# A decoder layer on one core: the slot-table product one shared block sooner, the last shared block in the regular loop, five gathers set around the last two gates

## What is computed

```python
x = layernorm(x + ssm(x))          # 32 heads of a gated state-space mixer
x = layernorm(x + by_id(x, ids))   # one of 4 small experts, chosen by token id
# third part, flat = x as 1024 x 256:
logits = flat @ gate_w.T
_, top_idx = top_k(logits + expert_bias, 2)
top_w = softmax(logits)[top_idx]; top_w /= top_w.sum()
for e in range(16):
    out += combine[:, e:e+1] * (silu(flat @ wg[e].T) * (flat @ wu[e].T)) @ wd[e].T
out += (silu(flat @ sw_gate.T) * (flat @ sw_up.T)) @ sw_down.T     # shared expert
x = layernorm(x + out)
```

## Time and profile before

| | us |
|---|---|
| median of 3 runs | 654.33 |
| lowest, highest | 653.83, 656.0 |
| the profiled execution | 655.03 |
| its span, first to last instruction | 653.3 |
| TensorE matmuls busy | 625.1 (96%) |
| DVE, ACT, POOL busy | 536.3, 453.1, 460.5 |

### The profile page before, as it was taken

How to read it: one execution, slowest core, us unless ns; L and a number is a source line. 1 busy time by engine, 2 the same in 40 slices (tenths; PEclk the granted TensorE clock), 3 DMA queues, 4 the chain that set the end, 5 groups by cost and what they waited for, 6 DMA issues and landing times.

```text
span 653.3 us, 12045 instructions
## 1 busy us (share of the span) xinstructions
PE 625.1 (96%) x3545; PEld 492.3 (75%) x3545; DVE 536.3 (82%) x874; ACT 453.1 (69%) x742; POOL 460.5 (70%) x439
## 2 busy tenths in 40 slices
PE   7989999999999999999999999999999999899990
PEld 6677888878888788887888878878889787655550
DVE  6999999999999999999999999985975477742245
ACT  3768797887888978879788797897522346533365
POOL 4395889879898798987989879858670551545554
PEclk9989999999999999999999999999999999999996
DMA  4261112121131211311113111122116279268745
GB/s 164 74 260 63 66 49 94 42 91 64 49 108 45 73 64 49 113 61 52 64 49 113 64 49 64 48 99 79 72 43 160 73 173 352 75 187 258 192 129 155
DMA packets 25993, 66.66 MB, mean 102 GB/s; under 512 B 4099, under 2 KB 16899, under 8 KB 23179
## 3 DMA queue, kind: packets, MB, share of 16 engines
q1 hardware_dynamic: 23131, 58.54, 26.7%
q0 software_dynamic: 2832, 7.75, 4.6%
HBM read 58.00 MB, written 9.85 MB: 104 GB/s over the span
## 4 chain that ended last, share of the span: by engine, by line
PE 89%; DVE 5%; ACT 2%; issue 2%; POOL 1%; DMA 1%; ACTq 0%; DVEq 0%
PE ps L871 38%; PE ps L885 9%; PE ps L901 7%; PE ps L1165 5%; PE ps L886 4%; PE ps L803 3%; PE ps L821 3%; DVE conv L1730 3%; PE ps L1214 3%; PE ps L845 2%; PE ps L1155 2%; PE ps L1071 2%; PE ps L1049 1%; PE ps L910 1%; PE ps L1189 1%
## 5 line engine op out<-in xcount | busy, mean ns | idle before, releaser
L1730 DVE SCALAR_TENSOR_TENSOR conv<-ps,w_raw,conv 128x506 f32<-128x506 f32 (+3 forms) x352 | 320.7, 934 | 15.7 <-ACT conv L1373 9.4
L871 PE MATMUL ps<-x_hi,w_hi 128*128 128x512 f32 x384 | 158.9, 414 | 2.7 <-DVE x_lo L1651 1.6
L1373 ACT ACTIVATE conv<-ps,w_raw 128x512 f32<-128x512 f32 x160 | 108.4, 688 | 65.1 <-PE ps L871 64.7
L871 PE MATMUL ps<-x_hi,w_lo 128*128 128x512 f32 x384 | 151.8, 395 | 0.0
L871 PE MATMUL ps<-x_lo,w_hi 128*128 128x512 f32 x384 | 150.7, 392 | 0.0
L532 POOL TENSOR_TENSOR decay<-cum_b,cum_tok 128x512 f32<-128x512 f32 (+1 forms) x128 | 103.3, 829 | 9.1 <-DMA cum_b<-cum_scratch 9.1
L871 PEld LDWEIGHTS ps<-x_hi,w_hi 128*128 128x128 f32 x384 | 72.7, 189 | 20.8 <-issue 2.4
L538 POOL TENSOR_TENSOR decay<-decay,mask 128x512 f32<-128x512 f32 x64 | 82.7, 1292 | 5.0
L871 PEld LDWEIGHTS ps<-x_hi,w_lo 128*128 128x128 f32 x384 | 72.4, 189 | 17.0 <-DVE w_lo L1656 0.2
L871 PEld LDWEIGHTS ps<-x_lo,w_hi 128*128 128x128 f32 x384 | 72.9, 190 | 12.8
L1358 ACT ACTIVATE conv<-conv 128x1024 f32<-128x1024 f32 x80 | 79.3, 1058 | 1.5 <-DVE conv L1730 1.5
(11 more groups left out here) (289 smaller groups left out, 1077.4 us busy)
## 6 DMA issues: line engine op xcount, KB each, us to landing
cum_b<-cum_scratch SPq DMA_DIRECT2D x16, 1024.0 KB, 4.6
w_raw<-in_winT SPq DMA_DIRECT2D x15, 778.0 KB, 4.3
y_all<-in_wgu SPq DMA_DIRECT2D x4, 1408.0 KB, 12.7
late<-in_wdn SPq DMA_DIRECT2D x2, 1408.0 KB
x_scratch<-conv SPq DMA_DIRECT2D x19, 128.0 KB, 6.2
late<-in_woutT SPq DMA_DIRECT2D x1, 2048.0 KB, 9.4
ys_scratch<-y_blk SPq DMA_DIRECT2D x32, 64.0 KB
res_scratch<-conv SPq DMA_DIRECT2D x11, 130.0 KB
```

Source lines behind the costliest of these rows:

```text
L871: mm = pe.matmul(ps[:, tile_bank(n, tile) + hf, :], wp[:, par, w], xp[:, kk, t], start=(i == 0), stop=(i == 5))
L1373: act.activation(conv[:, par, tile, hf * 512:(hf + 1) * 512], ps[:, tile_bank(n, tile) + hf, :], ACT.Copy, scale=w_raw[:, par, tap:tap + 1 ...
L1730: dve.scalar_tensor_tensor(out=o[:, :, s:], in0=u[:, :, 0:T - s], scalar=w_raw[:, par, c:c + 1], in1=o[:, :, s:], op0=ALU.mult, op1=ALU.ad ...
```

## The change

TensorE and ACT treat item 10 in the loop: gate_up(10) and silu_gate(10) come ahead of down(8) and take_y(8). slot_table() comes after gate_up(8) in place of gate_up(9). POOL issues gathers 0 and 1, gate 9, gather 2, gate 10, gather 3 (behind the end of down(8)), gather 4 (behind turn_hidden(10)); the wait for gate_up(10) ahead of gather 3 is gone.

```diff
             pool.wait_ge(S["st_x2"], 16 * TBS)
             gather_block(0)
+            gather_block(1)
             gate_shared(TBS - 2)
-            gather_block(1)
             gather_block(2)
-            pool.wait_ge(S["gu_done"], TBS)
+            gate_shared(TBS - 1)
+            pool.wait_ge(S["dn_done"], TBS - 2)
             gather_block(3)
-            gate_shared(TBS - 1)
+            pool.wait_ge(S["ht_done"], TBS)
             gather_block(4)
             pool.wait_ge(S["gu_done"], TBS + 1)
             gather_block(5)
...
-            for i in range(3, TBS - 1):
+            for i in range(3, TBS):
                 gate_up(i)
                 if i == 3:
                     ranks()
-                if i == TBS - 2:
+                if i == TBS - 3:
                     slot_table()
                 down(i - 2)
                 turn_hidden(i - 1)
-            down(TBS - 3)
-            turn_hidden(TBS - 2)
-            gate_up(TBS - 1)
             turn_block(TBS)
             down(TBS - 2)
...
-            for i in range(3, TBS - 1):
+            for i in range(3, TBS):
                 silu_gate(i)
                 take_y(i - 2)
                 take_hidden(i - 1)
                 if i == 6:
                     lanes_in_block()
-            take_y(TBS - 3)
-            take_hidden(TBS - 2)
-            silu_gate(TBS - 1)
             take_block(TBS)
             take_y(TBS - 2)
             take_hidden(TBS - 1)
```

## The result

The changed kernel takes 651.73 us in the median of 9 runs (650.81 to 652.45), the kernel before 653.83 us in its 9 runs of the same comparison (653.23 to 656.0): 2.10 us less, a ratio of 0.997 with a 95% interval of 0.9958 to 0.9982. The interval excludes "no change": it puts the gain at 1.2 to 2.7 us. It lies just about at the 0.3% that I had set as the bound of what can be told. The forecast was 652.4 us, made from the first three runs of before (654.33); the gain in it was 1.9 us, with 1.98 us for the stage from gate_up(8) to the first expert product.

A forecast was written before the change was run, and what follows sets the result against it. TensorE's waits for POOL's gate product (1.6 us) and ACT's copy (0.5) delay the first expert product. Steps from gate_up(8) sum to 10.03 us, formerly 12.01: 1.98 gained, 1.9 with the register load; 654.33 becomes 652.4 us, range 651.4 to 653.9.

The forecast's parts named there:

- What bounds it: Shared blocks before the expert part: whatever brings the first expert product (570.80 us) forward reaches the tail whole.
- The table: Table product after gate_up(8): no wait foreseen, 0.0 us to spare for first matmuls; table starts 2.27 us sooner.
- rival (c): Table product at its new place waits for DVE's comparisons; 0.3 us late leaves 1.6 us gain, 652.7 us; chance 0.12.
- The sign that I had named for (c): In the changed kernel's profile, a table product longer than 0.85 us would show it waiting for DVE.
- down(9): TensorE's down product of block 9 starts 1.77 us after down(8), including a new wait of about 0.46 us for ACT.
- The register load: read_expert(0), between down(9) and turn_hidden(10): 0 to 0.35 us may show; 0 in the sum, 0.1 in the forecast.
- POOL: POOL's new order: gather 0 at 561.76, gate 9 at 564.25, gate 10 done about 567.1, wanted at 568.25 us.
- Rival (b): DVE holds POOL's four instructions before gate 10 by 0.68 us each: gain 0.8 us, 653.5 us; chance 0.10.
- the sign "over 1.1 us": In the changed kernel's profile, POOL gates or gathers over 1.1 us would show that DVE holds POOL.
- Rival (d): Gather 3 lands only after SP's eleven residual stores; second pair's transposes wait 3.9 us: 656.3 us, slower; chance 0.05.
- The size: Total time: a 1.9 us gain on the three-run median of 654.33 gives 652.4 us, 0.29% less.
- The chances: Verdict on total time against a bound of about 0.3% (2.0 us): faster 0.42, same 0.52, slower 0.06.

## Why the prediction was right, point by point

*What bounds it.* That whatever brings the first expert product forward reaches the end held: the stage's 2.01 us, the 2.09 up to TensorE's last product and the medians' 2.10 agree.

*The table.* Expected without a wait at its new place, which rival (c) doubted: no wait, 0.88 us. DVE's comparisons ended at 558.62 (555.93+2.69), 0.12 us ahead of the product at 558.74, where I had seen 0.02. The margin is real but thin, as the kernel with the table one block sooner shows. The sign that I had named for (c), a product longer than 0.85 us, was set wrong: it took 0.88 us before as well.

*down(9).* The term that I had put together from two other places, 1.77 us from down(8), was 565.97-564.20 = 1.77. It appears as 0.30 us of idle time in the profile, not as 0.46, since idle time is counted from the modelled end of the transposition.

*The register load.* It didn't show: down(9) to turn_hidden(10) took 0.96 us (0.97). The 0.35 us that I had named as its upper bound don't follow from their terms (0.68+0.3 against 0.97 of cover leave 0.01). The 0.1 us that I had set aside for it in the forecast was not needed: the stage took 10.00 us, the sum without it said 10.03.

*POOL.* Measured from gate_up(8)'s start, gather 0 came at 3.06 us (2.97 foreseen), gate 9 at 5.56 (5.46), gather 2 at 6.29 (6.18), gate 10 at 7.74 (about 7.7), gather 3 at 8.52 (8.5), gather 4 at 10.12 (10.0). The queue never set TensorE's pace.

*Rival (b), POOL held by DVE.* My reading of the trace of before was wrong. DVE's tensor_scalar, 0.68 us beside gather 0 before, took 0.18 now (L2023), again beside gather 0, and gather 0 took 1.06 us both times: the two didn't hold each other. The 0.68 us come back only in the three traces of kernels with the loop but without the early table, in which, as before, gate 9 follows gather 0 at once. Of the four POOL instructions ahead of gate 10 none was held by 0.68 us: gather 1 took 1.11 us where it was 0.99, gate 9 0.58 (0.56). Since gather 3 took 1.14 us before, the sign "over 1.1 us" could not tell (b) either. The gate ended 1.1 us ahead of its use. DVE's start, 560.96 in the text of (b), should read 561.06 (563.33-2.27); nothing hangs on it.

*Rival (d), the residual stores.* They came at 564.85, 7.4 us after gate_up(8) (7.7 foreseen), and gathers landed 2.7 to 3.7 us after issue among them, where the rival's threshold was 7.3.

*The size.* The forecast of 652.4 lies 0.7 us over the result. 0.5 of it is the starting point: three runs of before gave 654.33, nine 653.83. The other 0.2 are the register load's 0.1 and 0.1 by which the medians differ by more than the stage. With an interval of 1.2 to 2.7 us for the gain, that the medians agree with the stage to 0.1 us is luck in part. What I had not priced is that the wait of 1.6 us that the change takes away is of a kind behind which the clock fell in two other traces, at 1.8 us each time. If that happens to the kernel before, the change is worth more than the stage shows; how often it does is open.

The chances put faster at 0.42 and no change at 0.52. With the result on the bound itself that was as near as the spread of the runs allowed; the stage had been known better than that.

## What to carry to other kernels

Three moves that are worth 0.8, 0.0 and -0.1 us alone were worth 2.0 together, because each removed one of three things that a single step (the last gate) waited for in turn: its gathers' data, its queue, its input. Before judging such a move alone, follow the step that is late back through all of them, and write down when each would be there. A wait to be removed is best measured from one step's start to the next one's, in one trace; spans of two traces differed by twice the effect.

## What the runs showed of the hardware that I had not expected

Behind a wait of TensorE of 1.6 to 1.8 us in an otherwise dense part the granted clock fell to 0.50 in two of the three traces of kernels with the loop but without the early table (the trace of before, with the same wait, has it at 1.00), and cost 1.8 us. Behind one wait of 1.55 us near 40 us, the same in all 14 traces, it fell in two, which cost 1.26 us in the one that was compared. So two executions of the same code can differ by over 1 us through the clock alone. A gather of 128 rows of 1 KB from DRAM was usable 2.8 us after POOL began to issue it where its user waited for it among SP's stores, and 2.9 us without them; but it took 4.4 us in one trace and 5.1 in another.
